# A 16-head sparse attention stage regrouped into quads of heads, one tile of 128 queries at a time

## The reference

```python
def _L1_attn_ref(hidden_states, W_attn, b_attn, W_proj, b_proj):   # N_HEAD = 16, STRIDE = 128, C = 8
    ...
    strided = cols % STRIDE >= STRIDE - C
    local = cols[None, :] // STRIDE == rows // STRIDE
    layout = (strided[None, :] | local) & (cols[None, :] <= rows)
    ...
    qkv = hidden_states @ W_attn + b_attn
    q, k, v = jnp.split(qkv, 3, axis=-1)          # 16 heads of 8 features each
    scores = jnp.einsum('bhqd,bhkd->bhqk', q, k) * scale
    attn = jax.nn.softmax(jnp.where(mask, scores, mask_value), axis=-1)
    out = jnp.einsum('bhqk,bhkd->bhqd', attn, v)
    return out.transpose(0, 2, 1, 3).reshape(B, S, E) @ W_proj + b_proj
```

## Time and profile before

| | us |
|---|---|
| median of three runs | 1316.31 |
| profiled execution | 1315.41 |
| its span, first to last instruction | 1313.3 |
| TensorE busy in it | 1174.5 |
| VectorE busy | 740.4 |
| ScalarE busy | 697.4 |
| GpSimd busy | 154.6 |

### The profile page before, as it was taken

One profiled execution on the slowest core, in us unless ns is written; L12 is line 12 of the kernel. 1 busy time (PEld: TensorE's weight loads), 2 busy tenths in 40 slices (PEclk: granted clock), 3 DMA queues, 4 the chain that ended last, 5 costly groups with the idle time before them and its releaser, 6 DMA issues.

```text
span 1313.3 us, 21926 instructions
## 1 busy us (share of the span) xinstructions
PE 1174.5 (89%) x7325; PEld 776.8 (59%) x7325; DVE 740.4 (56%) x1890; ACT 697.4 (53%) x1881; POOL 154.6 (12%) x272
## 2 busy tenths in 40 slices
PE   3789989997889998998798999999879999899967
PEld 2563775554765585555486468555557648655546
DVE  5542666677643375667754256567764426666651
ACT  3361676654553286565455157566545518655624
POOL 4310220001120121000212012000022002100000
PEclk9899999999899999999799999999989999999989
DMA  7300000000000000000000000000000000000000
GB/s 229 102 1 0 1 0 1 23 3 1 1 11 1 0 0 1 1 25 1 1 2 10 1 0 1 1 1 25 1 1 9 1 0 0 1 1 1 1 1 8
DMA packets 21058, 15.53 MB, mean 12 GB/s; under 512 B 872, under 2 KB 18645, under 8 KB 20957
## 3 DMA queue, kind: packets, MB, share of 16 engines
q1 hardware_dynamic: 20956, 14.24, 3.8%
HBM read 13.18 MB, written 1.05 MB: 11 GB/s over the span
## 4 chain that ended last, share of the span: by engine, by line
issue 56%; PE 31%; DVE 3%; POOL 3%; ACT 3%; POOLq 2%; SPq 1%; DVEq 0%; DMA 0%; ACTq 0%
PE ps L712 9%; PE ps L785 4%; PE ps L744 3%; PE ps L750 3%; PE ps L805 2%; PE ps L793 2%; POOL rstd L1428 2%; PE ps L725 1%; PE ps L613 1%; PE ps L781 1%; PE ps L646 1%; POOLq L1427 1%; PE ps L696 1%; SPq L440 1%; DVE lg_nmax L1710 1%
## 5 line engine op out<-in xcount | busy, mean ns | idle before, releaser
L1269 ACT ACTIVATE arena<-ps,nmax 128x512 f32<-128x512 f32 x256 | 176.2, 688 | 195.1 <-PE ps L877 176.1
L1860 DVE TENSOR_REDUCE nmax<-ps 128x1 f32<-128x512 f32 x256 | 164.4, 685 | 106.3 <-PE ps L866 106.3
L1078 ACT ACTIVATE arena<-ps 128x512 f32<-128x512 f32 (+6 forms) x304 | 170.3, 570 | 61.7 <-PE ps L467 13.8
L877 PEld LDWEIGHTS ps<-ident,arena 128*128 128x128 f32 x1024 | 110.2, 141 | 84.8 <-issue 48.1
L877 PE MATMUL ps<-ident,arena 128*128 128x128 f32 x1024 | 146.7, 282 | 5.1 <-ACT arena L1269 4.7
L1865 DVE COPY arena<-ps 128x512 f32<-128x512 f32 x128 | 87.6, 684 | 57.6 <-PE ps L877 57.4
L712 PE MATMUL ps<-big,w1a 128*128 128x512 f32 x256 | 117.3, 604 | 0.0
L1238 ACT ACTIVATE arena<-ps,snm 128x136 f32<-128x136 f32 x256 | 91.8, 375 | 5.8 <-DVE snm L1790 5.8
L1426 POOL TENSOR_TENSOR vare<-mv,eps_ln 128x2 f32<-128x2 f32 x64 | 13.5, 211 | 674.4 <-DVE mv L1539 673.8
L712 PEld LDWEIGHTS ps<-big,w1a 128*128 128x128 f32 x256 | 46.3, 189 | 57.5 <-issue 56.5
L785 PE MATMUL ps<-kT,arena 128*128 128x136 f32 x512 | 77.2, 279 | 0.0
(11 more groups left out here) (350 smaller groups left out, 2148.6 us busy)
## 6 DMA issues: line engine op xcount, KB each, us to landing
ctx<-in_ctx_dram SPq DMA_DIRECT2D x4, 512.0 KB, 4.8
w1a<-in_L_ffn_W_dram SPq DMA_DIRECT2D x1, 2048.0 KB, 10.0
w1b<-in_L_ffn_W_dram SPq DMA_DIRECT2D x1, 2048.0 KB, 11.9
w2b<-in_L_ffn_W_dram SPq DMA_DIRECT2D x8, 256.0 KB, 6.5
X<-in_x_dram SPq DMA_DIRECT2D x4, 256.0 KB, 3.6
out_dram<-Y SPq DMA_DIRECT2D x4, 256.0 KB, 2.4
arena<-in_L_xattn_Wq_dram SPq DMA_DIRECT2D x1, 512.0 KB
arena<-in_L_xattn_Wk_dram SPq DMA_DIRECT2D x1, 512.0 KB
```

Of the source, the lines that this page charges most:

```text
L877: last = pe.transpose(ps[:, 4 + h, k * P:(k + 1) * P], cprob[:, h, k * P:(k + 1) * P], ident[:, :])
L1078: return act.activation(dst, src, ACT.Copy)
L1269: act.activation(cprob[:, h, :], bank(2 * (t % 2) + h), ACT.Exp, bias=nmax[:, s:s + 1], accum_out=rsum[:, j % 2, s:s + 1]).then_inc(c_exp, 1)
L1860: dve.tensor_reduce(nmax[:, s:s + 1], bank(s % 4), AX.X, ALU.max, negate=True)\
```

## The change

The stage works by quads. A quad is one tile t of 128 queries and four neighbouring heads, numbered q = 4 t + s with s the 32-row slice of qT in which the four heads lie; 16 quads a pass, two at a time, written out with no inner loop.

- Keys are masked in place of queries: kTm[:, i] is kT with only head i of each slice kept, i = 0 to 3 (two by VectorE, two by ScalarE). One product of 32 rows, qT of the slice by the four masked copies, gives the scores of four heads, 512 columns, one PSUM bank. The causal mask is a bf16 product of 512 columns.
- The scores with the shared keys are taken once a pass (`shared_scores`), copied to G, and get their own maxima gnm, exponentials (`shared_exps`) and sums gsum. On second tiles `row_max` adds a drain and a minimum with gnm.
- The transposed probabilities are copied by VectorE, not ScalarE, into six buffers of spT. In a round VectorE's order is two copies, then two row maxima.
- The values are masked once, four copies Vm, by GpSimd. `values(t)` does 16 products with 32 columns of weights, each slice into its own 32 rows of bank 6, and for second tiles the product with the shared keys.
- The reciprocals are taken per tile: those of the first three tiles early (`inverse(0, TT - 1)`), transposed and copied before the last quads; the last tile's at the end.
- kTm and Vm lie in w1a. SyncE loads w1a anew in each of three passes, after the last values.

The diff, cut to its core:

```diff
-        qm = sparse_c(2, TOK)
-        SP_ = sparse_c(2, TT, KW)
-        spT = sparse_c(2, TOK)
+        SP_ = sparse_c(2, QH, P)
+        spT = sparse_c(6, QH, P)
...
+        kTm = w1a[:, 0:QH, :]
+        Vm = w1a[:, QH:2 * QH, :].rearrange("p i (t d) -> p i t d", d=D)
...
             with sp.Fori(0, ITERS - 1) as it:
+                sp.wait_ge(so_ps, it * TT + TT)
+                load_w1()
...
+                def two_masks(n):
+                    for q in (2 * n, 2 * n + 1):
+                        pe.matmul(bank(q % QUADS), ident_bf[:, :], causal[:, :].unsqueeze(1).to_broadcast([P, QH, P]),
+                                  start=True, stop=False)
+
+                def two_scores(n):
+                    for q in (2 * n, 2 * n + 1):
+                        t = q // QUADS
+                        pe.matmul(bank(q % QUADS), qT[strip(q), t * P:(t + 1) * P],
+                                  kTm[strip(q), :, t * P:(t + 1) * P], start=False, stop=True).then_inc(s_ps, 1)
...
+                def turn_probs(q):
+                    pe.wait_ge(s_exp, it * NQ + q + 1)
+                    if q == 0:
+                        pe.wait_ge(gs_read, it + 1)
+                    if q >= 2:
+                        pe.wait_ge(sT_ready, it * NQ + q - 1)
...
+                def values(t):
...
+                    for i in range(QH):
+                        for q in range(t * QUADS, (t + 1) * QUADS):
+                            last = pe.matmul(ps[strip(q), 6, t * P:(t + 1) * P], Vm[:, i, t, strip(q)],
+                                             spT[:, q % 6, i, :], start=(i == 0), stop=(i == QH - 1 and t % QT == 0))
...
+                for n in range(NQ // 2):
+                    if n in SHARED_AT:
+                        turn_shared(SHARED_AT.index(n))
+                    if n == NQ // 2 - 1:
+                        turn_inverse(0, TT - 1)
+                    turn_probs(2 * n)
+                    turn_probs(2 * n + 1)
+                    if n + 2 < NQ // 2:
+                        two_masks(n + 2)
+                        two_scores(n + 2)
+                    if n and n % 2 == 0:
+                        values(n // 2 - 1)
+                values(TT - 1)
+                turn_inverse(TT - 1, TT)
...
+                def exps(q):
+                    t = q // QUADS
+                    act.wait_ge(s_max, it * NQ + q + 1)
+                    if q >= 2:
+                        act.wait_ge(sT_ps, it * NQ + q - 1)
...
+                for n in range(NQ // 2):
+                    turned(2 * n)
+                    turned(2 * n + 1)
+                    if n + 2 < NQ // 2:
+                        row_max(2 * n + 4)
+                        row_max(2 * n + 5)
+                    if n == 1:
+                        shared_arg(0)
+                    if n == NQ // 2 - 3:
+                        shared_arg(1)
+                    if n == NQ // 2 - 2:
+                        inverse(0, TT - 1)
+                inverse(TT - 1, TT)
```

More of the change, by code:

```diff
@@ L809, in two_heads, with strip @@
[L809 to L822 removed]
+                def strip(q):
+                    return slice((q % QUADS) * 32, (q % QUADS + 1) * 32)
@@ new lines, in shared_scores @@
+                def shared_scores():
+                    for b in range(GROUP):
+                        t = b * QT + 1
+                        for q in range(QUADS):
+                            k0 = b * SEQ + P - CB
+                            last = pe.matmul(ps[:, 4 + q, b * QH * CB:(b + 1) * QH * CB],
+                                             qT[strip(q), t * P:(t + 1) * P], kTm[strip(q), :, k0:k0 + CB],
+                                             start=True, stop=True)
+                    last.then_inc(gs_ps, 1)
@@ L1255, in sparse_attention @@
-                act.wait_ge(gT_ps, it + 1)
-                copy(GT[:, :, :], ps[:, 4, 0:GROUP * P].rearrange("p (b q) -> p b q", b=GROUP)).then_inc(gT_ready, 1)
-                act.wait_ge(sinv_ps, it + 1)
-                copy(qT[:, :], bank(5)).then_inc(sinv_ready, 1)
+                act.wait_ge(qk_ready, it * 2 + 2)
+                for i in range(QH // 2, QH):
+                    last = act.activation(kTm[:, i, :], kT[:, :], ACT.Identity, scale=row_mask[:, i:i + 1])
+                last.then_inc(km_more, 1)
@@ new lines, in shared_exps, with shared_turned @@
+                def shared_exps(b):
+                    act.wait_ge(g_arg, it * GROUP + b + 1)
+                    act.activation(G[:, b, :, :], G[:, b, :, :], ACT.Exp).then_inc(g_exp, 1)
+                def shared_turned(b):
+                    act.wait_ge(gT_ps, it * GROUP + b + 1)
+                    copy(GT[:, b, :], ps[:, 7, b * P:(b + 1) * P]).then_inc(gT_ready, 1)
+                for q in range(NQ):
+                    exps(q)
+                    if q == NQ // 2 - 1:
+                        shared_exps(0)
+                    if q == NQ - 3:
+                        shared_exps(1)
+                    if q == NQ // 2 + 1:
+                        shared_turned(0)
@@ L1820, in sparse_attention @@
                 last.then_inc(xg_ready, 1)
[L1821 to L1825 removed]
+                dve.wait_ge(qk_ready, it * 2 + 2)
+                for i in range(QH // 2):
+                    last = dve.tensor_scalar(kTm[:, i, :], kT[:, :], row_mask[:, i:i + 1], None, ALU.mult)
+                last.then_inc(km_ready, 1)
                 dve.wait_ge(qkv_ps, it * 4 + 3)
```

251 lines of the change are left out of this document (108 added, 143 removed).

## The result

The changed kernel takes 1307.07 us (median of 6 runs, 1303.85 to 1310.63), the kernel before 1315.4 us beside it: ratio 0.9943, 95% interval 0.9919 to 0.9966. That is 0.57% or some 8 us less. The direction held, and the time lies in the wide range of 1284 to 1315, but outside the forecast's own range of 1286 to 1300: 20 us were forecast, under half of it came. The profiled execution is the longest of the six, 1310.63 us; its span is 1308.8 us, its mean granted clock 0.946 (before: 1313.3 us and 0.974).

A forecast was written before the change was run, and what follows sets the result against it. TensorE was taken as the bound, ScalarE close behind. Four passes of -6.8 (loop), +1.5 (head) and -0.1 (tail) made -21.6 us on 1315.41: 1294.7, taken as 1296; own range 1286 to 1300, wide range 1284 to 1315.

The forecast's parts named there:

- TensorE's new work: Sparse attention stage: transposes, masks, scores and values sum to 3.05 us per two quads, against 4.37 per two heads.
- Rivals 1 and 2: Score and value strips overlap only two at a time (1305 or 1314 us, 13%) or not at all (1345 or 1325, 8%).
- rival 1: Strips overlap only two at a time, values 1.71 us: 1305 us, or 1314 with slower scores too; chance 13%.
- The loop: Sparse stage, first to last exponential: 27.2 us, before 33.96; term -6.8 per pass.
- The head: Sparse stage, kT to first exponential: about 3.8 us, before 2.2; term +1.5 per pass.
- The tail: Sparse stage, last exponential to product with inverse sums: 4.3 us, before 4.4; term -0.1 per pass.
- This early move gains next to nothing: Tail: taking inverse sums early on VectorE, between copies of quads 13 and 14, was said to bring almost no gain.
- The reload: Three 2 MB reloads of w1a after the last value product: taken as 0 us, at most 30.
- rival 3: Sparse stage: the clock falls; 1340 us at 1.2 GHz throughout, 1300 to 1312 in a part; chance 10%.
- about 2 us for the O copy: Tail: sign of the forecast, TensorE waiting about 2 us for the O copy before quad 14.
- in a part of it 1300 to 1312: Milder case of the falling clock: 1.2 GHz in only part of the sparse stage, 1300 to 1312 us.
- a clock under 1.00 in the loop: Sign named in advance that the forecast is wrong: granted clock below 1.00 in the sparse stage's loop.

The follow-up runs named there:

- filled kernel: Changed kernel plus bf16 products whose results nobody reads, in TensorE's waits at head and tail: 1292.43 us, ratio 0.9832; without the early inverse sums 1295.03 us.
- the change in another order: Changed kernel, second sequence's shared exponentials behind quad 14, their transpose and the early inverse's behind quad 15's, no added products: 1292.61 us, ratio 0.9856.

## Why the prediction was right in direction and wrong in size

- **TensorE's new work** was sized right. Four strips overlap: values 1.01 us a tile (1.15 taken), scores 1.06 (1.06), 8 transposes 0.93 (0.98), 2 masks 0.53 (0.43, which the row of 0.12 for 272 columns would rather make 0.45). Rivals 1 and 2 are out. The Trainium skill (TensorE: Matmul & The Clock Gate, Part 3, What overlaps and what doesn't) says that products start and end in program order. The prediction drew from it the price of rival 1, 1.71 for the values. The 1.01 measured speaks against that inference and not against the page: the value records end in the order in which they start, 7 ns apart, and still lie side by side.
- **The loop**, at full clock, is 27.04 us from first to last exponential; 27.2 was forecast, the term 6.84 instead of 6.8. The waits named are there, for instance 1.2 us of ScalarE at shared_exps(1).
- **The head** is 3.88 us instead of 3.8: term +1.6, forecast +1.5.
- **The tail** at full clock is 4.0 us, forecast 4.3: term -0.5, forecast -0.1. "This early move gains next to nothing" was wrong by itself: it gives 1.0 us a pass (2.6 us in the time), which the filled kernels with and without it show.
- **The reload** costs nothing that the traces show, as taken.
- **The step that failed** is the sum's silent condition that every term runs at clock 1.00; it was set aside as rival 3. The runs showed 68 us at half clock that begin in the stage, in all four passes, worth 14.7 us in it in the profiled execution, and the gain back once TensorE's waits were filled. The prediction had found both idle stretches: it says that TensorE waits for the G copies and "about 2 us for the O copy", and priced them as waits alone, hidden behind other engines. It had the row that warned of it, clock 0.83 where TensorE was busy 12.94 of 20 us, and compared only the busy share of the whole stage (28 of 36 us), not the two stretches in which TensorE does nothing at all. The priced case "in a part of it 1300 to 1312" is what happened, and I gave the whole rival 10%. One of the prediction's own signs of being wrong, "a clock under 1.00 in the loop", came true: 0.51 from 153.50 to 166.50.

The account: 4 x 5.67 us a pass (40.6 less 34.93) makes 22.7 us, and the filled kernel is 22.9 us under the kernel before by the medians (1315.3 to 1292.4). The forecast had 21.6. Part of the agreement with the medians is luck: the spans of the two profiled executions differ by 24.9, and 2.7 of that lies outside the stage, between the passes (823.3 to 820.6), which no term of the sum holds and no run explains. In the profiled execution the falls took back 14.7 us inside the stage (6.3, 2.7, 3.4 and 2.3 over 34.9) and about 4 in what follows in passes 1 to 3: the stretches from OT to the next kT are 824.6 us together, 820.6 in the filled kernel. Together with 1.5 us behind the fourth pass, that is the difference of their spans, 1308.8 to 1288.4.

## What to carry to other kernels

When a change makes TensorE faster than its neighbours, look for the places where it will stand still in one piece (here 1.8 to 2.7 us), and price each as the wait plus a stretch at half clock behind it (here 1.0 to 4.7 us a fall in the loop), also where the wait is hidden. Work that is moved into such a wait (or another order, so that the waits become short and apart) can be worth more than the change itself: here the change in another order gave 22 us where the change as it was gave 8. And in a chain of engines that hand work to one another, what counts is which operation the next engine waits for: two copies behind two row maxima instead of ahead of them cost 69 us, with what the clock took in it.

## What the runs showed of the hardware that I had not expected

- The clock's fall is not settled by the length of the last idle stretch alone. Behind a wait of 2.68 us at the head it fell in 15 of 20 passes (five profiled executions), behind 1.93 to 1.94 us in 4 of 4, behind 0.70 us in none of 16; behind the 3.76 us put into the kernel before in 4 of 4. The five that held are pass 1 in four kernels and pass 4 in one. In the tail, 1.8 us and the 0.9 that follow went with a fall in 12 of 16 passes; in two more it came only in the next wait, of 1.16, and in two not at all. What else enters isn't shown by these runs, and stays open. Nor is it shown which of the tail's waits brings the clock down, since the kernels that fill them fill all at once.
- The fall's length differs as much: 13 us at half clock in pass 1 of the changed kernel, some 3 us in pass 2, with the same wait ahead of both. Runs of one kernel therefore differ, and follow their mean clock: the changed kernel's fastest run has 1303.85 us at 0.954, its slowest 1310.63 at 0.946.
- The clock fell behind a wait that costs nothing by itself, being hidden behind other engines: at full clock the loop takes 27.05 us with 2.68 us of it in the head and 27.04 with 0.70. It fell behind 1.94 and 1.83 us too, and in one kernel, in all four passes, behind 0.96 and 0.74 us with 0.7 us of transposes between them. In another kernel the same two waits went with a fall in one pass of four.
- Four products into four strips of 32 columns run side by side in f32: 16 products of 128 queries in 1.01 us. Two from strips of 32 rows and 512 columns take 1.06 us together.
